# Cross-attention and a nine-path FFN on one core: score tiles and maxima interleaved with P V in the first two steps, the second query, the weights' rounding and the early mix moved

## What is computed

```python
h = layernorm(x)
q = h @ Wq + bq                      # 16 heads of 16
k = ctx @ Wk + bk; v = ctx @ Wv + bv # one head of 16, shared
scores = where(mask == 0, -1e9, q k^T / 4)
x = x + softmax(scores) v @ Wo + bo
h = layernorm(x)
m = mix[0]*h[t-1] + mix[1]*h[t] + mix[2]*h[t+1]
paths = (m @ W1[p] + b1[p]) @ W2[p] + b2[p]        # p in 0..8
best = argmax(tanh(m @ Wo1 + bo1) @ Wo2 + bo2)
x = x + layernorm(h + paths[best]) * gamma + beta
```

## Time and profile before

| what | value |
|---|---|
| median of 3 executions | 334.41 us (333.69 to 335.15) |
| the profiled execution | 333.89 us |
| its span in the profile | 332.1 us |
| mean granted TensorE clock | 0.982 of full speed |
| instructions | 7164 |
| bytes read from HBM, written | 8.51 MB, 4.19 MB |

### The profile page before, as it was taken

One profiled execution on the slowest core, in us unless ns is written; L12 is line 12 of the kernel. 1 busy time (PEld: TensorE's weight loads), 2 busy tenths in 40 slices (PEclk: granted clock), 3 DMA queues, 4 the chain that ended last, 5 costly groups with the idle time before them and its releaser, 6 DMA issues. The chain is left out here.

```text
span 332.1 us, 7164 instructions
## 1 busy us (share of the span) xinstructions
PE 301.6 (91%) x2764; PEld 227.6 (69%) x2764; DVE 265.0 (80%) x612; ACT 182.1 (55%) x282; POOL 218.5 (66%) x259
## 2 busy tenths in 40 slices
PE   1687899789999999999999999999999999999991
PEld 1564376365668767796779766796779677967890
DVE  2776799998779796989789796989399768695876
ACT  1364906734971677547852777357553655266620
POOL 0292065683296499966996499957886598629454
PEclk9999779999999999999999999999999999999996
DMA  8952020020002001200120010000100010001003
GB/s 227 221 106 80 2 79 3 0 82 0 3 12 69 2 0 65 80 2 3 65 73 8 0 54 14 1 2 0 65 2 1 3 64 2 2 0 65 0 3 126
DMA packets 20588, 13.16 MB, mean 40 GB/s; under 512 B 10114, under 2 KB 20427, under 8 KB 20555
## 3 DMA queue, kind: packets, MB, share of 16 engines
q1 hardware_dynamic: 18914, 12.14, 12.7%
q10 hardware_dynamic: 1640, 0.57, 0.8%
HBM read 8.51 MB, written 4.19 MB: 38 GB/s over the span
## 5 line engine op out<-in xcount | busy, mean ns | idle before, releaser
L1521 POOL TENSOR_TENSOR rs<-ve,halfneg 128x4 f32<-128x4 f32 x22 | 23.7, 1075 | 43.8 <-DVE ve L1164 43.8
L907 ACT ACTIVATE e<-ps 128x1024 f32<-128x1024 f32 x32 | 31.1, 1024 | 14.1 <-PE ps L584 14.1
L1201 DVE TENSOR_REDUCE mx<-ps 128x16 f32<-128x1024 f32 x32 | 38.0, 1216 | 0.3 <-PE ps L547 0.3
L1615 POOL TENSOR_TENSOR hml<-hs,hmh 128x512 fp32r<-128x512 f32 x28 | 35.0, 1280 | 4.4 <-ACT hmh L969 4.4
L709 PE MATMUL ps<-w2h,hmh 128*128 128x256 f32 (+1 forms) x140 | 35.0, 288 | 0.0
L710 PE MATMUL ps<-w2l,hmh 128*128 128x256 f32 (+1 forms) x140 | 34.1, 280 | 0.0
L620 PE MATMUL ps<-wo,osb 128*128 128x256 f32 x128 | 32.4, 400 | 0.2 <-DVE osb L1228 0.2
L1321 DVE TENSOR_TENSOR hs<-hs,ps 128x512 f32<-128x512 f32 x28 | 18.5, 682 | 16.6 <-PE ps L689 16.6
L1580 POOL TENSOR_TENSOR y<-xh2f,gms 128x256 f32<-128x256 f32 x24 | 20.4, 880 | 16.2 <-DVE xh2f L1173 16.2
L1546 POOL TENSOR_TENSOR x<-xin,bos 128x256 f32<-128x256 f32 x32 | 22.8, 745 | 11.0 <-DVE rDs L1219 10.3
L932 ACT ACTIVATE xh<-x,vb,rs 128x256 f32<-128x256 f32 x22 | 11.5, 591 | 31.5 <-POOL vb L1534 31.5
(11 more groups left out here) (174 smaller groups left out, 800.3 us busy)
## 6 DMA issues: line engine op xcount, KB each, us to landing
xin<-in_x SPq DMA_DIRECT2D x8, 512.0 KB, 3.9
out<-y SPq DMA_DIRECT2D x6, 512.0 KB, 2.9
min_<-in_mask_Bx1xSxS_ik SPq DMA_DIRECT2D x8, 128.0 KB, 3.9
hs<-in_L_ffn_W SPq DMA_DIRECT2D x2, 288.0 KB
hs<-in_L_ffn_W SPq DMA_DIRECT2D x1, 512.0 KB
out<-y SPq DMA_DIRECT2D x2, 256.0 KB, 2.1
out<-xin SPq DMA_DIRECT2D x2, 256.0 KB, 2.3
cst<-in_constants SPq DMA_DIRECT2D x1, 384.0 KB, 6.3
```

The lines of the kernel that those rows point to most:

```text
L907: nc.scalar.activation(e[:, 2 * i:2 * i + 2, :], ps[:, bank:bank + 2, :], ACT.Exp).then_inc(s_e, 1)
L1201: v.tensor_reduce(mx[:, k, :].rearrange("p (a h) -> p a h", a=2), ps[:, bank:bank + 2, :].rearrange("p a (h s) -> p a h s", s=SK), AX.X, A ...
L1521: g.tensor_tensor(ln[7][:, :], ln[6][:, :], halfneg[:, :], ALU.pow).then_inc(s_r, 1)
L1615: g.tensor_tensor(L.lo(m, r), L.selected(m, r), L.hi(m, r).bitcast(F32), ALU.subtract).then_inc(L.s_hl, 1)
```

## The change

In the steps without an FFN part (steps 1 and 2) the first two score tiles for the maxima go between the halves of P V and the denominators, and their maxima ahead of the reciprocal; the third goes behind the denominators, with its maximum between reciprocal and normalisation; only the fourth stays behind the spread. The banks are (6, 4, 6, 2). The query of (0,1) is made in step 1 behind the first transposed scores instead of in step 0. x_lo of step 0 goes behind the maxima. W1 is rounded at the end of step 0 and its remainder made at the start of step 1; W2's rounding goes ahead of the query's copy. The query is copied when the remainder of the query before is made (it waited for the scores), and it is rounded when the scores are made. Of the early mix of batch 0 the second half goes to the end of step 2 on VectorE, with its rounding in step 3 ahead of `copy_t2` and its remainder behind `rstd2` on GpSimd. The core of the diff:

```diff
-            return (6, 2) if n and not f else (2, 4)
+            return (6, 4, 6, 2) if n and not f else (2, 4, 2, 4)
...
+                ramp = banks[0] == 6
-                if banks[k % 2] == 2 and k < 2:
+                if banks[k] == 2 and (k < 2 or ramp):
                     pe.wait_ge(s_rd, at(b, NJ, j))
-                if banks[k % 2] == 4 and k < 2:
+                if banks[k] == 4 and k < 2 and not ramp:
                     pe.wait_ge(s_oT, at(b, 2 * NJ, 2 * j))
-                if banks[k % 2] == 6 and k < 2:
+                if banks[k] == 6 and k < 2:
                     pe.wait_ge(s_q, at(b, NJ * KD, (j + 1) * KD))
...
-            def pv(b, j, front, f):
+            def pv(b, j, front, f, banks):
...
-                mm.then_inc(s_o, 1)
+                    if half:
+                        mm.then_inc(s_o, 1)
+                    if not f:
+                        scores_for_max(*front, half, banks)
...
-            def spread(b, j):
+            def spread(b, j, front, f):
                 pe.wait_ge(s_rd, at(b, NJ, j + 1))
+                if not f:
+                    pe.wait_ge(s_mx, at(front[0], NJ * NT, front[1] * NT + 2))
...
                 if n:
                     scores_transposed(*n, 0, front)
+                if n == (0, 0):
+                    wq(*front, fb)
...
-                elif front:
+                elif n:
+                    scores_for_max(*front, 2, banks)
+                else:
                     scores_for_max(*front, 0, banks)
                     scores_for_max(*front, 1, banks)
...
                 elif front:
-                    scores_for_max(*front, 2, banks)
+                    if not n:
+                        scores_for_max(*front, 2, banks)
                     scores_for_max(*front, 3, banks)
-                if not n:
-                    wq(*after, fb)
```

ScalarE:

```diff
-            def split_ffn_weights():
+            def w1_high():
...
+            def w2_high():
...
             def q_copy(b, j, bank):
-                act.wait_ge(s_st, at(b, NJ * NPAIR, j * NPAIR))
+                act.wait_ge(s_ql, at(b, NJ * KD, j * KD))
...
             def q_round(b, j):
+                act.wait_ge(s_st, at(b, NJ * NPAIR, j * NPAIR))
...
                     softmax_exp(*n, 0)
+                if n and n == (0, 0):
+                    w2_high()
+                if late and f:
+                    early_mixed_hi(late[0], (1,))
+                if n and not f:
+                    q_copy(*front, 6)
...
-                if late:
-                    q_copy(*front, 0 if f else 6)
-                if n and n == (0, 0):
-                    split_ffn_weights()
+                if late and f:
+                    q_copy(*front, 0)
...
-                    early_mixed_hi(n[0])
+                    early_mixed_hi(n[0], (0,))
                 if not n:
                     copies_t1(*after, 6, False, 1)
+                    w1_high()
```

VectorE and GpSimd:

```diff
             def q_round(b, j):
+                dve.wait_ge(s_st, at(b, NJ * NPAIR, j * NPAIR))
...
+                if n and n == (0, 0):
+                    w1_lo()
                 if after:
                     layernorm1_stats(*after)
                 if n and n == (0, 0):
-                    ffn_weights_lo()
+                    w2_lo()
...
-                    early_mix(late[0])
+                    early_mix(late[0], (0,))
...
+                if front and not f:
+                    take_max(*front, 0, banks)
+                    take_max(*front, 1, banks)
                 if n:
                     invert(*n)
                 if front and not f:
-                    take_max(*front, 0, banks)
-                    take_max(*front, 1, banks)
-                if not n:
-                    x_lo(*after, 6)
+                    take_max(*front, 2, banks)
                 if n:
                     attn_normalise(*n)
...
-                    if front:
-                        take_max(*front, 2, banks)
-                        take_max(*front, 3, banks)
-                        split_max(*front)
+                    take_max(*front, 3, banks)
+                    split_max(*front)
                     if n:
                         x1_stats(*n, 0)
                         x1_stats(*n, 1)
+                    else:
+                        x_lo(*after, 6)
...
+                if late and not f:
+                    early_mix(late[0], (1,))
...
-                    early_mixed_lo(n[0])
+                    early_mixed_lo(n[0], (0,))
...
                     rstd2(*n)
+                if n and n[1] == NJ - 1 and not f:
+                    early_mixed_lo(n[0], (1,))
```

More of the change, by code:

```diff
@@ L539, in scores_for_max @@
                 ks = slice(k * P, (k + 1) * P)
-                bank = banks[k % 2]
+                bank = banks[k]
                 for a in range(2):
@@ L746, in step @@
                 if n:
-                    pv(*n, front, f)
+                    pv(*n, front, f, banks)
                 if f:
@@ L757, in step @@
                 if n:
-                    spread(*n)
+                    spread(*n, front, f)
                 if f:
@@ L939, in mixed_hi, with early_mixed_hi @@
                     nc.scalar.activation(xmh[:, c, j * CH:(j + 1) * CH], xm[:, c, :], ACT.Copy).then_inc(s_xmh, 1)
-            def early_mixed_hi(b):
-                for c in range(KD):
+            def early_mixed_hi(b, cs=range(KD)):
+                for c in cs:
                     act.wait_ge(s_early, at(b, KD, c + 1))
@@ L987, in step @@
                         softmax_exp(*n, 1)
-                    if front:
+                    if front and (f or not n):
                         q_copy(*front, 0 if f else 6)
@@ L1118, in layernorm2_apply, with w1_lo, w2_lo @@
                 a.then_inc(s_ln2d if upper else s_ln2, 1)
-            def ffn_weights_lo():
+            def w1_lo():
                 dve.wait_ge(s_w1h, 1)
                 v.tensor_tensor(w1l[:, :, :], w1_32, w1h[:, :, :].bitcast(F32), ALU.subtract).then_inc(s_w1l, 1)
+            def w2_lo():
                 dve.wait_ge(s_w2h, 1)
@@ L1242, in x1_stats, with mix @@
                     variance(ln2, (s_ln2s, s_ln2p, s_ln2v), c, 2 * c, -1.0)
-            def mix(b, j, last, sems):
+            def mix(b, j, last, sems, cs=range(KD)):
                 dve.wait_ge(s_x2T, at(b, NJ * KD, (j + 1) * KD))
-                for c in range(KD):
+                for c in cs:
                     n = at(b, KD, c + 1)
@@ L1265, in second_mix, with early_mix @@
                 mix(b, 1, CH, (s_mix1, s_mix2, s_xm))
-            def early_mix(b):
-                mix(b, 0, CH - 1, (s_early1, s_early2, s_early))
+            def early_mix(b, cs=range(KD)):
+                mix(b, 0, CH - 1, (s_early1, s_early2, s_early), cs)
             def last_column(b):
@@ L1567, in mixed_lo, with early_mixed_lo @@
                     g.tensor_tensor(xml[:, c, js], xm[:, c, :], xmh[:, c, js].bitcast(F32), ALU.subtract).then_inc(s_xml, 1)
-            def early_mixed_lo(b):
-                for c in range(KD):
+            def early_mixed_lo(b, cs=range(KD)):
+                for c in cs:
                     pool.wait_ge(s_earlyh, at(b, KD, c + 1))
```

## The result

The changed kernel takes 338.11 us (median of 4, 337.72 to 339.91) against 334.77 for the kernel before (4 executions): ratio 1.0115, 95% interval 1.0071 to 1.016. It is slower by 3.3 us where 0.7 us less was forecast, and outside the stated range. The profiled execution took 337.90 us, 4.0 more than that of before; its span is 336.1.

What follows compares the result with a forecast made beforehand. TensorE was taken to bound 90 to 330 us, with no single bound in the ramp before. The ramp's terms moved the first W1 product from 82.65 to 81.95, so 0.7 off the 334.41 median: 333.7 us, range 331.9 to 335.2.

Steps and rivals of the forecast that it cites:

- the first W1 product: Step 3, chunk (0,0): starts at 81.95 instead of 82.65 us, and this shift carries to the end one for one.
- it lay beside the maxima and cost nothing: Step 0: Wq of (0,1), 3.05 us on TensorE, cost no time there; it moves behind step 1's first scores.
- The split of step 0: Step 0: the maxima start 1.0 us earlier, so their split ends at 27.0 us.
- the 1.0 us that the forecast gave to x_lo's move: Step 0: x_lo no longer ahead of the third maximum lets the pair of maxima begin 1.0 us earlier, at 23.9.
- The clock rival: Step 1's projection: the low clock comes again, 1.06 us is not gained there, whole kernel 334.7 us; chance 0.17.
- The 8.1 us chain: Step 1, VectorE from reciprocal to split's end: one maximum leaves each side of the normalisation; split ends 2.2 us earlier, at 45.7.
- the casts of step 2: Step 2: the query's two casts fall beside GpSimd's score operands and take 1.4 us, ending at 60.0.
- Step 2's query: Step 2: score tile 0 and P V's second half wait for it until 60.6; most of the 2.2 us is given back.
- step 3's mix: Step 3: the second mix half takes 2.0 to 2.33 us on VectorE, making it late for the last column, 81.1 to 81.4.
- A tile ahead of the denominators: Steps 1 and 2: score tile 1 between P V's second half and the denominators adds 0.58 us (0.6 in step 2).
- The slower rival: Step 0, ScalarE: W1's rounding waits for the FFN loads and holds up the maxima; 336.5 us if complete at 29; chance 0.07.

Runs made afterwards that it cites:

- a2: Changed kernel, with GpSimd making the query's remainder only behind the split of the maxima in steps 1 and 2; 336.19 us, ratio 1.0045 to before.
- a4: Changed kernel, with VectorE rounding step 2's query ahead of the first half of the early mix; 337.27 us, ratio 1.0081 to before.
- a5: Changed kernel, with the early mix of batch 0 undivided in step 2 as before; 340.22 us, ratio 1.0163 to before.
- b1: Kernel before, with only the query of (0,1) moved behind the first transposed scores and x_lo behind the maxima; 335.79 us, ratio 1.0049.
- a1: Changed kernel, with the query of (0,1) back in step 0 and x_lo again ahead of the third maximum; 337.16 us, ratio 1.008 to before.
- a3: Changed kernel, with ten unread products of 512 columns filling TensorE's gap behind step 0's last score tile; 336.59 us, ratio 1.0067 to before.
- c1: Changed kernel with the three mends a1, a2 and a4 together; 333.77 us, ratio 1.0 to before.
- c2: c1, with the last column mixed ahead of the next LayerNorm's statistics on VectorE in step 3; 333.84 us, ratio 0.9979 to before.
- d1: c2, with VectorE rounding step 1's query ahead of W2's remainder; 333.64 us, ratio 0.9966 to before.
- d2: d1, with four unread products behind step 1's first scores and four behind the third score tile of steps 1 and 2; 332.05 us, ratio 0.9935.
- b2: Kernel before, with four unread products behind step 1's first scores and four between the first two tiles of steps 1 and 2; 333.59 us, ratio 0.9975.
- e1: Kernel before, with the change's score tiles, maxima, banks, query waits and weights' rounding; query of (0,1) in step 0, mix whole; 339.57 us, ratio 1.0158.

## Why the prediction was wrong

At the first W1 product the forecast was 4.75 us short; 3.9 of them were there when LayerNorm 2 of (0,0) began. In order of time: 1.43 at the end of step 0's split, 1.44 more at the first exponentials, 1.37 more over step 1's projection, 0.97 more between step 2's reciprocal and LayerNorm 2, and half a microsecond less in the stretches between.

- **Step 0, the term that failed: "it lay beside the maxima and cost nothing".** Wq's 3.05 us were priced as time, and rightly (they are now between the two sets of scores). What was not priced is what they did for TensorE where they were. Of the profiled kernels, the five with the gap (changed, a2, a4, a5, b1) all have a granted clock of 0.50 that begins in it or behind it, between 26.5 and 33.5 us; the nine with Wq or fillers in it (before, a1, a3, c1, c2, d1, d2, b2, e1) have none between 26 and 33, though four of them (before, a1, c2, e1) fall low between 33 and 38. It cost 1.5 us from split to exponentials in the changed kernel and in b1, and a3, which only fills the gap, gets 1.3 of them back. What it costs the whole is known less well: 1.5 us by a3's median, with overlapping intervals, and 1.3 in b1, where x_lo's move is in it too. The rule I put beside the projection, of the Trainium skill (TensorE: Matmul & The Clock Gate, What's actually happening), that activity lifts the clock, agrees with this; I asked it of the wrong gap.
- **The split of step 0** was forecast at 27.0 and came at 28.43, because the changed kernel's profiled execution was at the low clock from 22 to 25 us, ahead of the gap. This does not follow the change: a5, c1, d1, d2 and b2 have it too, before, a1, a2, a3, a4, b1, c2 and e1 do not, with nearly the same work up to there. From the first score tile to the end of the split 8.62 us pass in the changed kernel, 6.94 in a2 and 6.95 in a3; so it is 1.7 us of that one execution, and whether the other three had it isn't known. Before, it was 7.90: the 1.0 us that the forecast gave to x_lo's move was right.
- **The clock rival happened** in addition: 5.19 us for the projection of step 1 where 3.72 was forecast. I had given it 0.17. Among the kernels without filler ahead of that projection (all but d2 and b2) five of twelve show it there, and two in step 2's. It was 4.78 before too, so it explains little of the difference between the kernels (0.4 us) and much of the forecast's error (1.5). The argument for 2.4 GHz there, that the work was packed more tightly, was not enough.
- **The split beside the remainder was not seen.** The 8.1 us chain was shortened on paper without asking what it would fall on: GpSimd's remainder starts 2.8 us behind the inverse (in the profiles of before and changed alike, behind GpSimd's addition of x), and the split, earlier by one maximum, met it: 2.18 us (73.12 to 75.30) where c1 needs 0.75. In step 1 the slow projection hid it, in step 2 the statistics came 1.4 later. It accounts for the 0.97 above. For the casts of step 2 I had asked this question, and answered it by a row; 1.4 was forecast and 1.27 measured.
- **Step 2's query and step 3's mix were right in size.** The second half was forecast to start 1.5 us behind its exponentials and did so 1.4 behind (a4 takes it away); from LayerNorm 2 to the first W1 product the mix half costs 1.06 where 1.2 was forecast. A tile ahead of the denominators costs 0.7 (the reciprocals of the changed kernel follow the halves by 3.58 instead of 2.88), not 0.58.
- **The slower rival was the wrong mechanism.** W1's rounding ran at 24.82 to 26.09 and held nothing up, though the reading against it was too wide: the earlier trace rows show idle DMA engines only for 25.0 to 25.5, and from 26.0 to 28.5 they were at 0.68 in the kernel before, with the next inputs. (The FFN loads are fourteen, not fifteen.) A forecast whose likeliest sum was near nothing needed the clock as its slower rival, and for the gap that the change itself opened.

What stays open: of the executions that make up the medians only one per kernel has a profile. For the others the mean granted clock is known, and it is lower in the longer groups of c1 and d1, but not where in the ramp it fell. So the price of each single term in the median is not shown; that the three mends together pay for the loss is.

## What to carry to other kernels

Before work is moved out of a stretch where it "costs nothing", look at what its engine will do there instead: on TensorE an emptied wait can be paid for by the work behind it, at half the clock. When a chain on one engine is shortened, lay its new times beside the engine that it will now run together with (here GpSimd, beside which VectorE's split took 2.18 us instead of 0.75), and put a product that waits for another engine behind, not ahead of, work that is ready. And where the clock decides, compare spreads and several profiles, not one.

## What was not expected of the hardware

- **Products that nobody reads pay.** Eight in step 1 and four in step 2 of the kernel before (b2), 3.6 us of TensorE, take 1.0 us off its median (ratio 0.9975, 0.9957 to 0.9994) and shrink its spread from 3.1 (25 executions) to 1.0 us (12).
- **The split's operations end with GpSimd's.** The remainder's two operations took 72.48 to 75.02; the cast of the split took 0.78 instead of 0.29 and the subtraction 1.37 instead of 0.42, ending 0.3 behind GpSimd's second. The Trainium skill (SBUF — State Buffer, SBUF: two separate sides) calls this an exclusive lock held for the whole instruction; the subtraction agrees with that. The two casts of step 2's query, 1.27 us instead of 0.75, lost 0.52 beside operands of up to 0.96 us: that is within the rule, and far from the case of two whole operands.
- **A tile of another shape behind P V starts only when P V's half ends.** In steps 1 and 2 of every profile with the tiles there, the tile's first product starts 1.0 us behind the start of a P V half that takes 1.06 at 2.4 GHz, and 1.8 to 1.9 behind one that takes 1.9 at 1.2 GHz (step 2 of a5 and e1). The row of its weight load shows idle time with no wait for another engine; why it starts no earlier is not shown. In the changed kernel, step 1:

```profile
40.09 0.10 PEld L545 LDWEIGHTS ps<-cst,mT 64*128 64x128 bf16 x2 [0.84 <-issue]
```
